# Causal cover of the third and fourth query tile: from PE's cover products to one VectorE call with the row maximum

## The chip, the cores and the metric

The kernel runs on one core of one Trainium2 chip. The metric is the device time of one execution in microseconds (us). Before the change the three timed runs gave 1072.38, 1071.35 and 1063.21 us, median 1071.35 us.

## The reference, cut to what matters

The program computes one layer over 8 batches of 512 tokens with 128 features: a Mamba2 block with a residual and a layer norm, then causal attention with 16 heads of width 8, then a mixture of eight experts with two chosen per token, and layer norms. The change touches the scores of the attention alone:

```
scores = jnp.einsum('bhqd,bhkd->bhqk', q, k) / jnp.sqrt(jnp.float32(hd))
causal = jnp.tril(jnp.ones((s, s), bool))
scores = jnp.where(causal, scores, jnp.finfo(scores.dtype).min)
attn = jax.nn.softmax(scores, axis=-1)
```

A query row may look at itself and at earlier keys. The softmax needs the largest allowed score of each row, and this maximum is what the changed code finds.

## The kernel before, in words

The stages follow one another with barriers between them: the Mamba stage, the projection to queries, keys and values, attention (`attention_layer`, about 326 to 797 us of the profile), the experts and the last norms. `layer` calls them in this order.

In attention a batch has 512 queries, which are 4 query tiles of 128, and 16 heads in 4 groups of four. The scores are computed twice. First the **maximum pass**: PE multiplies 128 queries of one head with the keys up to the end of their tile, into one of four PSUM banks (`S_BANK`), and VectorE takes the maximum along each row into `mx`. `MAX_UNITS` lists the work of a pass, 11 units for each group of heads: tile 0 is one unit of four heads (4 times 128 columns), tile 1 two units of two heads (2 times 256), tiles 2 and 3 four units each with one head (384 and 512 columns). A pass has 44 units (`NMAX`), of which 32 have one head. Then, after all 44, PE transposes the maxima (`max_rows`, line 1619), VectorE splits them into three bf16 parts (lines 1429 to 1436), and SyncE stores these parts by DMA into rows of `qx` (`store_max`, line 1168). Second the **exponential pass** of the same batch: PE multiplies again, transposed and with the maxima as more rows (line 1632), ScalarE takes the exponential (line 1353), GpSimd sets what the causal mask forbids to zero (line 1313), PE multiplies with the values (`pv`, line 1647).

`SCHEDULE` sets the order of all engines around this: 44 slots, one unit of the exponential pass of a batch in each, and between them, up to slot 35, the units of the maximum pass of the *next* batch. Further steps of the batch *before* have slots of their own, among them its layer norm (lines 1453 to 1469) and the choice of its experts (`choose`, lines 1480 to 1528, a chain of 21 small VectorE instructions in slots 21 to 32, each of which waits for the one before; PE's `ranks`, line 1688, waits for one of them). Slot 36 holds the transposition of the maxima. Every engine works through its own queue in order and waits at semaphores.

The maximum pass of batch 0 stands alone in front of the loop and uses six banks instead of four. The seven other passes are woven into the exponential passes of batches 0 to 6. The exponential pass of batch 7 has no maximum pass beside it.

A unit's cover: for each head PE adds a second product to the block on the diagonal (line 1614), the 128 by 128 identity times `hide`, which holds -3e38 above the diagonal and zero elsewhere. So the forbidden scores are hidden before VectorE's `tensor_reduce` (line 1417) sees them. PE waits in front of unit u of a pass until VectorE has done unit u-4 (`mx_ready`), so that the bank is free.

In the loop an instruction that has to wait carries a wait on a register's value. `wait_apart` puts the wait into an instruction of its own, with a semaphore increment behind it.

Of the kernel before, what the change touches and what calls it, by code (L numbers as in the profile page):

```python
# [5 lines left out]
BF16 = mybir.dt.bfloat16  # L6
U32 = mybir.dt.uint32
ALU = mybir.AluOpType
# [3 lines left out]
P = 128  # L12
BATCH, SEQ, D = 8, 512, 128
# [35 lines left out]
def wait_apart(eng, sem, value, passed):  # L49

    eng.wait_ge(sem, value)
    eng.sem_inc(passed, 1)
# [786 lines left out]
QK_ROWS = PARTS * PARTS * DH  # L839
# [157 lines left out]
NMAX, NEXP, STEPS = len(MAX_UNITS), len(EXP_UNITS), GROUPS * TILES  # L997
# [46 lines left out]
def attention_layer(nc, x1_dram, q_parts, k_parts, v_dram, w_o, g1, b1, wg, w1, w2, slots, h_all, gates, table, w1s, w2s):  # L1044
# [6 lines left out]
    with ExitStack() as ctx:  # L1051
        def sb(name, shape, dt=F32):
            return ctx.enter_context(nc.sbuf_tensor(name, shape, dt))

        def pair(name, shape, dt=F32):
            return [sb(f"{name}{p}", shape, dt) for p in range(2)]

        def sem(name):
            sems.append(nc.alloc_semaphore(name))
            return sems[-1]  # L1060
# [5 lines left out]
        ident = sb("ident_c", [P, P])  # L1066
        ident16 = sb("ident16", [P, P], BF16)
        hide = sb("hide", [P, P], BF16)
        minus_half = sb("minus_half_c", [P, TILES])
        qx = pair("qx", [96, AH, SEQ], BF16)  # L1070
        kx = pair("kx", [96, AH, SEQ], BF16)
# [3 lines left out]
        mx = sb("mx", [P, AH, TILES])  # L1075
# [37 lines left out]
        ps = ctx.enter_context(nc.psum_tensor("psB", [P, 8, 512], F32))  # L1113
        S_BANK, E_BANK, PV_BANK, MISC = 0, 4, 6, 7

        S_BANKS, E_BANKS, FIRST_BANKS = 4, 2, 6

        w_loaded, consts, vx_made = sem("wo_loaded"), sem("att_constants"), sem("vx_made")
        kones_made, kones_loaded = sem("kones_made"), sem("kones_loaded")
        qk_loaded, v_loaded, vx_ready = [[sem(f"qk_loaded{p}_{g}") for g in range(GROUPS)] for p in range(2)], [sem(f"v_loaded{p}") for p in range(2)], sem("vx_ready")  # L1120
        s_ps, mx_ready = sem("s_ps"), sem("mx_ready")
# [14 lines left out]
        pool_passed, dve_passed, pe_passed = sem("pool_passed_c"), sem("dve_passed_c"), sem("pe_passed_c")  # L1136
# [4 lines left out]
        def times(it, p):  # L1141

            return it + p // 2 + 1
# [87 lines left out]
        def spread_v(pool, it, p):  # L1231
            q = p % 2
            wait_apart(pool, v_loaded[q], times(it, p) * 16, pool_passed)
            nc.gpsimd.tensor_copy(vx[q][:, :, :, 0:DH], vtok[q][:, :, :].rearrange("p t (h d) -> p t h d", d=DH)).then_inc(vx_ready, 1)

        @block.gpsimd
        def _(pool):
# [5 lines left out]
                                    pattern=[[-1, P]], channel_multiplier=1).then_inc(consts, 1)  # L1243
            nc.gpsimd.affine_select(out=ident16[:, :], in_=ones[:, :], compare_op=ALU.is_equal, fill=0.0, base=0,
                                    pattern=[[-1, P]], channel_multiplier=1).then_inc(consts, 1)
            nc.gpsimd.affine_select(out=hide[:, :], in_=hide[:, :], compare_op=ALU.is_gt, fill=0.0, base=0,
                                    pattern=[[1, P]], channel_multiplier=-1).then_inc(consts, 1)
            pool.wait_ge(vx_made, 2)
            spread_v(pool, 0, 0)
            nc.gpsimd.memset(ones16[:, :], 1.0).then_inc(route_consts, 1)  # L1250
# [5 lines left out]
                                    pattern=[[1, P]], channel_multiplier=-1).then_inc(route_consts, 1)  # L1256
# [76 lines left out]
            for e in range(E):  # L1333
                nc.gpsimd.indirect_dma_start(out=slots, out_offset=bass.IndirectOffsetOnAxis(ap=fill_idx[:, e:e + 1], axis=0),
                                             in_=filler[:, :], in_offset=None, bounds_check=SLOTS - 1,
# [69 lines left out]
        def _(dve):  # L1405
# [7 lines left out]
            def max_unit(row, u, banks=S_BANKS):  # L1413
                qt, h0, heads = MAX_UNITS[u]
                width = (qt + 1) * P
                dve.wait_ge(s_ps, row(NMAX, u + 1))
                nc.vector.tensor_reduce(mx[:, h0:h0 + heads, qt],  # L1417
                                        ps[:, S_BANK + u % banks, 0:heads * width].rearrange("p (h n) -> p h n", n=width),
                                        AX.X, ALU.max).then_inc(mx_ready, 1)
# [53 lines left out]
            def choose(it, p, i):  # L1473
# [53 lines left out]
                    ins = v.tensor_tensor(gates[:, 1, row_tiles(it, p)], gates[:, 0, row_tiles(it, p)], ex[:, :], ALU.mult)  # L1527
                ins.then_inc(chosen, 1)

            for u in range(NMAX):  # L1530
                max_unit(Row(0, 0), u, FIRST_BANKS)
            max_rows(Row(0, 0), 0, 0)
# [42 lines left out]
            for e in range(E):  # L1575
# [14 lines left out]
                                        op0=ALU.mult, op1=ALU.add))  # L1590
# [7 lines left out]
        def _(pe):  # L1598
            pe.wait_ge(consts, 6)

            def max_unit(row, it, p, u, banks=S_BANKS):

                qt, h0, heads = MAX_UNITS[u]
                q, width = p % 2, (qt + 1) * P
                if u % (NMAX // GROUPS) == 0:
                    pe.wait_ge(qk_loaded[q][h0 // 4], times(it, p) * QK_LOADS)
                n = row(NMAX, u + 1 - banks)
                if not isinstance(n, int) or n > 0:
                    pe.wait_ge(mx_ready, n)
                for j in range(heads):  # L1610
                    out = ps[:, S_BANK + u % banks, j * width:(j + 1) * width]
                    nc.tensor.matmul(out, qx[q][0:QK_ROWS, h0 + j, qt * P:(qt + 1) * P],  # L1612
                                     kx[q][0:QK_ROWS, h0 + j, 0:width], start=True, stop=False)
                    ins = nc.tensor.matmul(out[:, qt * P:width], ident16[:, :], hide[:, :], start=False, stop=True)  # L1614
                ins.then_inc(s_ps, 1)
# [608 lines left out]
def layer(nc, X, W_in, conv_w, conv_b, dt_bias, A_log, Dskip, norm_w, W_out,  # L2224
          w_qkv, w_o, g1, b1, wg, w1, bb1, w2, bb2, g2, b2, out):

    def dram(name, shape, dt=F32):
        return nc.dram_tensor(name, shape, dt, kind="Internal").ap()

    x1 = dram("x1_rows", (BATCH, SEQ, D))  # L2230
    q_parts = dram("q_parts", (BATCH, PARTS, D, SEQ), BF16)
    k_parts = dram("k_parts", (BATCH, PARTS, D, SEQ), BF16)
    v = dram("v_rows", (BATCH, SEQ, D))
    slots = dram("slots", (SLOTS, PAY))
    results = dram("results", (RESULTS, D))

    mamba_layer(nc, X, W_in, conv_w, conv_b, dt_bias, A_log, Dskip, norm_w, W_out, x1)
    qkv_projection(nc, x1, w_qkv, q_parts, k_parts, v)
    with ExitStack() as kept:
        gates = kept.enter_context(nc.sbuf_tensor("gates", [P, TOPK, ALL_TILES], F32))  # L2240
        table = kept.enter_context(nc.sbuf_tensor("table", [1, 3, SLOT_TILES], U32))
        h_all = kept.enter_context(nc.sbuf_tensor("h_all", [P, ALL_TILES, D], F32))
        w1s = kept.enter_context(nc.sbuf_tensor("w1s", [P, E * F], F32))
        w2s = kept.enter_context(nc.sbuf_tensor("w2s", [P, E * F], F32))
        attention_layer(nc, x1, q_parts, k_parts, v, w_o, g1, b1, wg, w1, w2, slots, h_all, gates, table, w1s, w2s)
        x1s = kept.enter_context(nc.sbuf_tensor("x1s", [P, ALL_TILES, D], F32))
        experts(nc, slots, w1s, bb1, w2s, bb2, table, results, x1, b2, x1s)
        last_norms(nc, x1s, h_all, results, gates, g2, out)
# [22 lines left out]
```

## Time and profile before

| what | us |
|---|---|
| median of three runs | 1071.35 |
| the profiled execution | 1066.94 |
| its span, first to last instruction | 1065.3 |
| PE busy over the span | 759.3 |
| VectorE busy over the span | 652.5 |
| ScalarE busy over the span | 505.2 |
| GpSimd busy over the span | 394.0 |
| all cover products on PE (512) | 113.1 |
| all row maxima of 512 columns with one head (128) | 82.5 |
| all row maxima of 384 columns (128) | 65.6 |

Matmuls overlap in PE's pipeline, so the busy time of a group is not what it takes from the queue: the distance from one start to the next is. The same holds for VectorE, in a smaller measure. "Idle before" is charged to the instruction that had to wait, with the engine and line that released it.

### The profile page before, as it was taken

What the parts mean: (1) busy time and instruction counts of PE and PEld (TensorE: products, weight loads), DVE (VectorE), ACT (ScalarE), POOL (GpSimd) and SP (SyncE); (2) the same over time, 40 slices, a digit from 0 to 9 for tenths busy, and PEclk for the clock granted to TensorE, in tenths of its full rate; (3) what the DMA queues carried; (4) which work ended last, traced back from release to release, by engine and by line L of the source; (5) the groups of instructions that cost most, each with busy time, mean ns of one, the idle gap of its engine ahead of it and who ended that gap; (6) DMA issues with size and microseconds to landing.
All of it is one profiled execution on the core that took longest, in us unless ns stands there. A gap on an engine that the chain in (4) does not pass through costs nothing. (4 is left out here: it accounts for less than half of the span.)

```text
span 1065.3 us, 21410 instructions
## 1 busy us (share of the span) xinstructions
PE 759.3 (71%) x5297; PEld 506.3 (48%) x5298; DVE 652.5 (61%) x1639; ACT 505.2 (47%) x987; POOL 394.0 (37%) x500
## 2 busy tenths in 40 slices
PE   5788887777564589989788979898820799998000
PEld 3565666555342334535354434443320699998000
DVE  3888887885355546768486938692231355554485
ACT  3556555552260035556455635555500566765134
POOL 1223332233200012353435343545535355555254
PEclk9989988987695558999899969997855799999555
DMA  1000000000284311344424232301201332221231
GB/s 43 16 21 26 25 15 14 25 15 11 89 264 150 120 33 47 86 104 98 119 65 111 74 100 66 96 24 50 65 30 38 88 85 72 82 83 32 82 114 43
DMA packets 87086, 72.38 MB, mean 68 GB/s; under 512 B 10932, under 2 KB 78139, under 8 KB 87007
## 3 DMA queue, kind: packets, MB, share of 16 engines
q1 hardware_dynamic: 81726, 60.29, 20.4%
q0 software_dynamic: 5280, 11.13, 3.3%
q8 instruction: 39, 0.64, 0.3%
q14 instruction: 41, 0.33, 0.1%
HBM read 44.05 MB, written 22.12 MB: 62 GB/s over the span
## 5 line engine op out<-in xcount | busy, mean ns | idle before, releaser
L1353 ACT ACTIVATE pb<-psB 128x512 f32<-128x512 f32 (+1 forms) x352 | 187.2, 558 | 205.9 <-PE psB L1632 175.5
L1417 DVE TENSOR_REDUCE mx<-psB 128x1 f32<-128x384 f32 (+3 forms) x352 | 209.4, 635 | 108.8 <-PE psB L1614 105.8
L1612 PE MATMUL psB<-kx,qx 72*128 72x384 bf16 (+3 forms) x512 | 150.3, 344 | 21.7 <-DMA kx<-k_parts 21.7
L1632 PE MATMUL psB<-qx,kx 75*128 75x256 bf16 (+3 forms) x512 | 136.0, 326 | 37.4 <-DMA qx<-mparts 18.4
L1313 POOL TENSOR_SCALAR_AFFINE_SELECT pb<-pb 128x512 f32<-128x512 f32 x128 | 81.3, 641 | 185.8 <-ACT pb L1353 184.5
L1647 PE MATMUL psB<-pb,vx 128*32 128x512 f32 (+3 forms) x1024 | 107.2, 494 | 14.1 <-POOL pb L1313 14.1
L1614 PE MATMUL psB<-hide,ident 128*128 128x128 bf16 x512 | 113.1, 244 | 0.0
L1632 PEld LDWEIGHTS psB<-qx,kx 75*128 75x128 bf16 x512 | 45.5, 103 | 123.3 <-issue 62.6
L1883 POOL DMA_INDIRECT results<-y_e,dest x72 | 70.1, 974 | 77.7 <-DVE y_e L1950 39.1
L1943 DVE TENSOR_TENSOR pre<-psE,biases 128x512 f32<-128x512 f32 x72 | 49.8, 692 | 55.8 <-PE psE L1981 42.6
L1989 PE MATMUL psE<-w2s,gT 128*128 x576 | 80.0, 282 | 2.9 <-ACT gT L1912 1.4
L1300 POOL DMA_INDIRECT slots<-pay,idx x64 | 64.3, 1005 | 45.3 <-DVE den_r L1523 14.9
L1981 PE MATMUL psE<-hT_e,w1t 128*128 128x128 f32 x576 | 77.6, 279 | 0.3 <-ACT hT_e L1907 0.3
L1612 PEld LDWEIGHTS psB<-kx,qx 72*128 72x128 bf16 x512 | 56.7, 111 | 41.2 <-issue 25.2
L1989 PEld LDWEIGHTS psE<-w2s,gT 128*128 128x128 f32 x576 | 69.7, 191 | 7.4 <-issue 6.2
L277 POOL TENSOR_TENSOR ra<-upto,a 128x512 f32<-128x512 f32 x32 | 34.5, 1090 | 104.2 <-DVE a L515 104.2
L1981 PEld LDWEIGHTS psE<-hT_e,w1t 128*128 128x128 f32 x576 | 71.1, 195 | 0.9 <-ACT hT_e L1907 0.7
L1614 PEld LDWEIGHTS psB<-hide,ident 128*128 128x128 bf16 x512 | 57.6, 112 | 21.0 <-issue 7.4
L1902 ACT ACTIVATE w1t<-w1s 128x512 f32 x72 | 45.4, 630 | 44.3 <-DMA biases<-in_L_ffn_bb 38.9
L1912 ACT ACTIVATE gT<-pre 128x512 f32<-128x512 f32 x72 | 45.4, 630 | 37.8 <-DVE pre L1943 22.3
L481 DVE SCALAR_TENSOR_TENSOR acc<-psA,cw,acc 128x509 f32<-128x509 f32 (+2 forms) x72 | 53.7, 746 | 5.1 <-ACT acc L348 3.4
L201 PE MATMUL psA<-xdt,mm 128*128 128x64 f32 x256 | 36.8, 291 | 20.7 <-DVE mm L549 20.7
(246 smaller groups left out, 1328.6 us busy)
## 6 DMA issues: line engine op xcount, KB each, us to landing
qx<-q_parts SPq DMA_DIRECT2D x96, 96.0 KB
kx<-k_parts SPq DMA_DIRECT2D x96, 96.0 KB
hin<-slots SPq DMA_DIRECT2D x72, 64.5 KB
ys<-results SPq DMA_DIRECT2D x16, 256.0 KB, 3.0
q_parts<-qpart SPq DMA_DIRECT2D x8, 384.0 KB
k_parts<-kpart SPq DMA_DIRECT2D x8, 384.0 KB
xin<-in_L_attn_X SPq DMA_DIRECT2D x8, 256.0 KB
x_rows<-x1o SPq DMA_DIRECT2D x8, 256.0 KB
```

Of the source, the lines that this page charges most:

```text
L481: ins = nc.vector.scalar_tensor_tensor(out=acc[:, c, s:SEQ], in0=bank(6 + c % 2)[:, 0:SEQ - s], scalar=cw[:, c, k:k + 1], in1=acc[:, c, s: ...
L1300: nc.gpsimd.indirect_dma_start(out=slots, out_offset=bass.IndirectOffsetOnAxis(ap=idx[q][:, k, t:t + 1], axis=0), in_=pay[k][q][:, t, :], ...
L1313: nc.gpsimd.affine_select(out=pb[step % PBUF][:, :, 0:P], in_=pb[step % PBUF][:, :, 0:P], compare_op=ALU.is_ge, fill=0.0, base=0, pattern= ...
L1353: nc.scalar.activation(pb[step % PBUF][:, h0:h0 + heads, 0:width], src, ACT.Exp).then_inc(exp_ready, 2 if u == NEXP - 1 else 1)
L1417: nc.vector.tensor_reduce(mx[:, h0:h0 + heads, qt], ps[:, S_BANK + u % banks, 0:heads * width].rearrange("p (h n) -> p h n", n=width), AX. ...
L1612: nc.tensor.matmul(out, qx[q][0:QK_ROWS, h0 + j, qt * P:(qt + 1) * P], kx[q][0:QK_ROWS, h0 + j, 0:width], start=True, stop=False)
L1614: ins = nc.tensor.matmul(out[:, qt * P:width], ident16[:, :], hide[:, :], start=False, stop=True)
L1632: ins = nc.tensor.matmul(ps[:, E_BANK + u % E_BANKS, j * width:(j + 1) * width], kx[q][0:MAX_ROWS, 4 * g + h0 + j, kt * P:(kt + 1) * P], q ...
L1647: ins = nc.tensor.matmul(ps[32 * j:32 * (j + 1), PV_BANK, kt * P:SEQ], vx[q][:, kt, 4 * g + j, :], pb[step % PBUF][:, j, 0:width], start=( ...
L1883: nc.gpsimd.indirect_dma_start(out=results, out_offset=bass.IndirectOffsetOnAxis(ap=dest[tile.ring][:, 0:1], axis=0), in_=y[tile.ring][:, ...
L1981: ins = nc.tensor.matmul(ps[:, UP_BANK + tile.pair, c * P:(c + 1) * P], w1t[tile.pair][:, c * P:(c + 1) * P], hT[tile.pair][:, :], start=T ...
L1989: ins = nc.tensor.matmul(ps[:, Y_BANK + tile.pair, 0:D], gT[tile.pair][:, c, :], w2s[:, bass.ds(at + c * D, D)], start=(c == 0), stop=(c = ...
```

## The change

For the units with one head (query tiles 2 and 3) PE no longer adds the cover product: there is one matmul per unit, which ends the accumulation. VectorE's `tensor_reduce` is replaced by `tensor_tensor_reduce`, which adds `cover` to the scores, writes the sums as bf16 to a scratch tile `covered`, and gives the maximum of the sums in `mx`. `cover` is a new fp32 tile of 128 by 512 in SBUF, zero where a key is allowed and -3e38 elsewhere, of which the last 384 or all 512 columns are read. GpSimd makes it at the stage's start. Its wait on PE becomes a `wait_apart`. Units with four or two heads are unchanged, so `hide` stays.

```diff
+        cover = sb("cover", [P, SEQ])
...
+        covered = [sb(f"covered{k}", [P, SEQ], BF16) for k in range(FIRST_BANKS)]
...
+            nc.gpsimd.memset(cover[:, :], 0.0).then_inc(cover_made, 1)
+            pool.wait_ge(cover_made, 1)
+            nc.gpsimd.affine_select(out=cover[:, :], in_=cover[:, :], compare_op=ALU.is_ge, fill=-3e38, base=SEQ - P,
+                                    pattern=[[-1, SEQ]], channel_multiplier=1).then_inc(cover_made, 1)
             pool.wait_ge(vx_made, 2)
...
             def max_unit(row, u, banks=S_BANKS):
                 qt, h0, heads = MAX_UNITS[u]
                 width = (qt + 1) * P
+                if heads == 1:
+                    wait_apart(dve, s_ps, row(NMAX, u + 1), dve_passed)
+                    nc.vector.tensor_tensor_reduce(out=covered[u % banks][:, 0:width], in0=ps[:, S_BANK + u % banks, 0:width],
+                                                   in1=cover[:, SEQ - width:SEQ], scale=1.0, scalar=-3e38, op0=ALU.add, op1=ALU.max,
+                                                   accum_out=mx[:, h0, qt:qt + 1]).then_inc(mx_ready, 1)
+                    return
...
+            dve.wait_ge(cover_made, 2)
             for u in range(NMAX):
                 max_unit(Row(0, 0), u, FIRST_BANKS)
...
                     pe.wait_ge(mx_ready, n)
+                if heads == 1:
+                    nc.tensor.matmul(ps[:, S_BANK + u % banks, 0:width], qx[q][0:QK_ROWS, h0, qt * P:(qt + 1) * P],
+                                     kx[q][0:QK_ROWS, h0, 0:width], start=True, stop=True).then_inc(s_ps, 1)
+                    return
```

On VectorE, in the loop, among the steps that choose the experts of the batch before (`lg`, `m`, `key` and `kmax` belong to that choice; REGISTER_ALU computes the value that a wait compares with), there stood before:

```order
L1416 REGISTER_ALU
L1417 TENSOR_REDUCE mx<-psB 128x1
L1480 REGISTER_ALU
L1495 SCALAR_TENSOR_TENSOR lg<-sel,lg 128x32
L1480 REGISTER_ALU
L1498 TENSOR_REDUCE m<-lg 128x4
L1416 REGISTER_ALU
L1417 TENSOR_REDUCE mx<-psB 128x1
```

The same place with the change (line 1425 is the new call, 1508 and 1511 are the two steps of the choice):

```order
L51 REGISTER_ALU
L1425 ISA covered,mx<-psB,cover 128x512
L1425 ISA mx 128x1
L1493 REGISTER_ALU
L1508 SCALAR_TENSOR_TENSOR lg<-sel,lg 128x32
L1493 REGISTER_ALU
L1511 TENSOR_REDUCE m<-lg 128x4
L51 REGISTER_ALU
L1425 ISA covered,mx<-psB,cover 128x512
L1425 ISA mx 128x1
```

The order of the steps is the same. One call stands as two instructions on VectorE: one that reads the scores and `cover`, and one that has no input and writes `mx`.

On PE at the same slots (line 1632 is a product of the exponential pass) there stood before:

```order
L1609 REGISTER_ALU
L1612 MATMUL psB<-kx,qx 128x512
L1614 MATMUL psB<-hide,ident 128x128
L1630 REGISTER_ALU
L1632 MATMUL psB<-qx,kx 128x384
L1609 REGISTER_ALU
L1612 MATMUL psB<-kx,qx 128x128
L1614 MATMUL psB<-hide,ident 128x128
```

and with the change:

```order
L1623 REGISTER_ALU
L1625 MATMUL psB<-kx,qx 128x512
L1648 REGISTER_ALU
L1650 MATMUL psB<-qx,kx 128x384
L1623 REGISTER_ALU
L1630 MATMUL psB<-kx,qx 128x128
L1632 MATMUL psB<-hide,ident 128x128
```

The product with `hide` is gone behind the 512-column unit and stays behind the 128-column ones; nothing else moved.

## Rows read from the trace of the kernel before

**Rows 1.** The page: busy time over the span, and PE's granted clock by slices.

```profile
PE 759.3 (71%) x5297; PEld 506.3 (48%) x5298; DVE 652.5 (61%) x1639; ACT 505.2 (47%) x987; POOL 394.0 (37%) x500
PEclk9989988987695558999899969997855799999555
```

**Rows 2.** Busy time in stretches: start:end, length, then each engine, clock, DMA.

```profile
core 0: us, PE busy (x) PEld busy (x) DVE busy (x) ACT busy (x) POOL busy (x), PEclk, DMA share, GB/s
573.00:614.60 41.60, 37.94 (x342) 20.49 (x342) 33.78 (x84) 23.35 (x46) 17.89 (x24) 0.96 0.38 98
626.00:672.60 46.60, 43.45 (x341) 22.46 (x341) 34.07 (x84) 22.96 (x46) 14.11 (x20) 0.83 0.30 80
377.00:421.20 44.20, 43.96 (x284) 21.62 (x285) 27.56 (x48) 21.05 (x39) 8.16 (x13) 0.67 0.12 35
```

**Rows 3.** Timeline of VectorE, 573 to 615 us: start, length, instruction, [idle before].

```profile
584.23 1.29 DVE L1417 TENSOR_REDUCE mx<-psB 128x1 f32<-128x512 f32 x2 [0.91 <-PE psB L1614]
596.76 1.29 DVE L1417 TENSOR_REDUCE mx<-psB 128x2 f32<-128x512 f32 x2 [0.39 <-PE psB L1614]
598.63 0.56 DVE L1417 TENSOR_REDUCE mx<-psB 128x1 f32<-128x384 f32 x1 [0.58 <-PE psB L1614]
603.48 0.19 DVE L1489 TENSOR_TENSOR key<-key,rank 128x32 f32<-128x32 f32 x1
603.59 1.28 DVE L1417 TENSOR_REDUCE mx<-psB 128x1 f32<-128x512 f32 x2
608.33 0.56 DVE L1417 TENSOR_REDUCE mx<-psB 128x1 f32<-128x384 f32 x1 [0.55 <-PE psB L1614]
611.98 2.47 DVE L1417 TENSOR_REDUCE mx<-psB 128x1 f32<-128x512 f32 x4
```

**Rows 4.** Timeline of PE at the end of the same pass.

```profile
612.28 0.22 PE L1614 MATMUL psB<-hide,ident 128*128 128x128 bf16 x1
614.60 0.27 PE L1619 MATMUL psB<-ident_c,mx 128*64 128x128 f32 x1 [0.38 <-issue]
```

**Rows 5.** Timeline of PE from the maxima of the pass before to the next exponentials.

```profile
567.42 0.27 PE L1619 MATMUL psB<-ident_c,mx 128*64 128x128 f32 x1 [0.38 <-DVE mx L1417]
573.06 0.39 PE L1632 MATMUL psB<-qx,kx 75*128 75x512 bf16 x1 [0.75 <-DMA qx<-mparts]
```

**Rows 6.** Timeline of PE: a cover product at the full clock, then at half of it.

```profile
603.20 0.22 PE L1614 MATMUL psB<-hide,ident 128*128 128x128 bf16 x1
603.26 0.33 PE L1632 MATMUL psB<-qx,kx 75*128 75x384 bf16 x1
...
382.09 0.31 PE L1614 MATMUL psB<-hide,ident 128*128 128x128 bf16 x1
382.20 0.53 PE L1612 MATMUL psB<-kx,qx 72*128 72x384 bf16 x1
```

**Rows 7.** Timeline, first pass: VectorE's last step, SyncE's stores, PE's first exponential.

```profile
362.12 0.28 DVE L1436 TENSOR_TENSOR mparts<-mrest,mparts 64x128 bf16<-64x128 f32 x1
364.62 0.43 SPq L1162 DMA_DIRECT2D vtok<-v_rows  x1
365.09 4.41 SPq L1168 DMA_DIRECT2D qx<-mparts  x3
377.24 0.59 PE L1632 MATMUL psB<-qx,kx 75*128 75x512 bf16 x1 [16.05 <-DMA qx<-mparts]
```

**Rows 8.** Timeline of VectorE: two-source instructions of 512 columns, PSUM with SBUF.

```profile
317.48 0.68 DVE L952 SCALAR_TENSOR_TENSOR qrest<-psB,qpart 128x512 f32<-128x512 f32 x1
318.08 0.68 DVE L952 SCALAR_TENSOR_TENSOR krest<-psB,kpart 128x512 f32<-128x512 f32 x1
```

**Rows 9.** Timeline of ScalarE in the Mamba stage: sums read out of its accumulator.

```profile
54.97 0.19 ACT L408 ACTIVATION_READ_ACCUMULATOR sq<-y 128x1 f32 x1
55.19 0.42 ACT L408 ACTIVATE sq<-y 128x256 f32<-128x256 f32 x1
55.52 0.19 ACT L408 ACTIVATION_READ_ACCUMULATOR sq<-y 128x1 f32 x1
55.61 1.00 ACT L413 ACTIVATE yT<-psA 128x1024 f32<-128x1024 f32 x1
```

**Rows 10.** Timeline at the stage's start: GpSimd's last constant, and VectorE's first maxima.

```profile
326.94 0.29 POOL L1246 TENSOR_SCALAR_AFFINE_SELECT hide<-hide 128x128 bf16<-128x128 bf16 x1
336.20 24.45 DVE L1417 TENSOR_REDUCE mx<-psB 128x4 f32<-128x512 f32 x44 [4.93 <-PE psB L1614]
```

**Rows 11.** Timeline of VectorE: an instruction behind a wait that stands apart (line 1460).

```profile
586.27 0.87 DVE L1457 BATCH_NORM_STATS2 bst_c<-r_c 128x6 f32<-128x128 f32 x4
587.28 0.38 DVE L1462 BATCH_NORM_AGGREGATE mv_c<-bst_c 128x2 f32<-128x6 f32 x4
```

More of the change, by code:

```diff
@@ L1116, in attention_layer @@
         S_BANKS, E_BANKS, FIRST_BANKS = 4, 2, 6
+        covered = [sb(f"covered{k}", [P, SEQ], BF16) for k in range(FIRST_BANKS)]
         w_loaded, consts, vx_made = sem("wo_loaded"), sem("att_constants"), sem("vx_made")
+        cover_made = sem("cover_made")
         kones_made, kones_loaded = sem("kones_made"), sem("kones_loaded")
```

## The prediction

> **What bounds the kernel now.** I read the page first. Over the span no engine is full [rows 1], so the change has to be judged stage by stage. It lies in attention, and there I asked for busy time by stretches, one for each maximum pass in the loop. A typical pass runs from a first exponential at 573.06 to the transposition of the maxima at 614.60 [rows 4, 5]. In these 41.6 us PE is busy 37.94 and VectorE 33.78 [rows 2]: near each other, with ScalarE and GpSimd far behind. A PE busy 91% looks like the bound, but a matmul's record is longer than its place in the queue, so I went on to VectorE's timeline. Up to 584.23 it waits for PE again and again, the last time for 0.91 us. In the 30 us from there to the end it waits three times, 0.39, 0.58 and 0.55 us, 1.52 together [rows 3]. At the end PE has finished the last unit's cover by 612.50, while VectorE still has four reduces from 611.98 to 614.45. PE's transposition starts at 614.60, behind VectorE, after only 0.38 us of idleness of its own [rows 3, 4]. The reader is to see that **VectorE sets the end of the pass, with PE close behind**. What follows hangs on that end: from transposition to the next batch's first exponential it is 5.64 us, the last part of it a wait for the stored maxima [rows 5]. A microsecond more on VectorE before the transposition is a microsecond more in the kernel.
>
> **The sum, part by part.** Per pass 32 units change.
>
> *PE's cover products go.* Start to start one takes 0.06 us at the full clock and 0.11 at half [rows 6]. In the typical pass they are 32 x 0.06 = 1.9 us, but not of the path: PE's work already ends before VectorE's. There I count nothing for them beyond fewer waits of VectorE (below). In the first pass of the loop, 377 to 421 us, PE is busy 43.96 of 44.20 and VectorE only 27.56 [rows 2]. This one is PE's. Half of its changed units run at the low clock, half after the clock has risen: 16 x 0.11 + 16 x 0.06 = **-2.7 us**.
>
> *VectorE's main instruction.* Four reduces of 512 columns last 2.47 us with 0.68 for the last, so 0.60 from start to start [rows 3]. Two-source instructions of the same width, one source in PSUM, one in SBUF, also start 0.60 apart [rows 8]. I take no difference, and 0.02 as its upper end.
>
> *VectorE's second instruction*, the reading of the accumulator into `mx`, is new: the call is not one instruction but two. VectorE does no such reading in this trace. The nearest rows: a small VectorE instruction of 32 columns delays the reduce behind it by 0.11 [rows 3]. The 128 columns between 384 and 512 make some 0.12 (records of 0.56 and 0.68), so 32 columns are 0.03 of it and one column leaves **0.08**. ScalarE does read an accumulator. There 0.22 passes from the reading's start to the next instruction where that waits for it, 0.09 where it does not [rows 9]. So 0.22 is my upper end. The lower is zero, since records of 0.68 already overlap by 0.08. I take 0.08, because the next unit's main instruction waits for nothing of the reading.
>
> The Trainium skill ("Vector Engine (DVE) Microarchitecture Reference", Measured stream behaviour on trn2) gives about 75 ns per instruction beside the columns. By that the sum below would be about 0.6 us smaller, so it would not change sign.
>
> *The wait that stands apart.* Behind the one VectorE has before (line 1460), 0.14 us lie between the end of the statistics and the next start [rows 11], where reduces whose scores are there follow without a gap. In the dense part the wait is met before its turn comes and runs beside the streaming instruction, so nothing. Where VectorE waits for PE it may add 0.1, and there it has slack. If it were paid in the dense part it would act like a larger second instruction.
>
> *A typical pass.* Six of the 32 changed units lie before 584.23 and vanish in waits for PE. The 26 behind it lengthen VectorE by 26 x 0.08 = 2.1 us. Against this stand the 1.52 us of waits. Part of them stays, since PE comes late there for steps that themselves wait for VectorE (norm and choice of the batch before), so I let half, 0.8, absorb. That is **+1.3 us**. Five passes are of this kind (2, 3, 4, 5 and 7): **+6.5 us**. Pass 6 (626 to 672.6) ran in part at a low clock and has VectorE idle for 46.60 - 34.07 = 12.5 us [rows 2]. Its second half is as dense as the others, so I take **+0.5**.
>
> *The first pass, alone, is covered.* VectorE runs 44 reduces without a break [rows 10] and would take 32 x 0.08 = 2.6 us longer. But its last step ends at 362.40, and SyncE stores the maxima only at 365.09, after the loads of batch 1 queued ahead. That is 2.7 us of cover. Then the stores land at 377, behind those loads' traffic [rows 7]. **0**. GpSimd's two instructions for `cover` start at 327.2, nine microseconds before the first reduce [rows 10]. A quarter of that work took 0.29, so it is free. The added wait passes at once.
>
> Sum: -2.7 + 6.5 + 0.5 = **+4.3 us**. Against the profiled execution (1066.9) that is 1071. That execution lies 4.4 us under the median and about 1.6 under the mean of all four times shown (1068.5), and I put the kernel on that mean: **1073 us**.
>
> **The rivals.**
>
> *The reading waits for its predecessor to drain (slower).* Then each unit costs 0.22, and 0.02 for the main one: 26 x 0.24 - 0.8 = 5.4 us per pass, 27 for five, about 3 for pass 6, -2.7 for the PE pass, and 32 x 0.24 - 2.7 = 5.0 in the first pass, most of it still behind the loads: +27 to +32, or 1096 to 1101. The place is the dense half of each pass. For it: ScalarE's rows with the wait. Against: those without. With a cost c per unit the change reaches +1% (10.7 us, about what a measurement of this kernel can tell from no change) at c near 0.13. The Trainium skill ("VectorE: DVE Perf Modes", The DRAIN you can't avoid) says the next instruction does not start until the pipe is empty, and its rules advise few instructions. That speaks against this change. Records of 0.68 that start 0.60 apart disagree in part, and no row here shows it for a reading. Chance that the cost is large enough, between 0.13 and 0.24: **0.36**.
>
> *PE sets the passes (faster).* Then every product counts: 32 x 0.06 = 1.9 in five passes, 2.4 in pass 6, 2.7 in the PE pass, 14.7 us in all: 1054. For it: 91% busy. Against: VectorE's dense half and the last reduce. The skill ("Trainium Kernel Development and Optimization", Performance Expectations) calls PE's matmul time a bad measure and its weight loads a good one; these are 20.49 of 41.60 [rows 2], on the side of the forecast. Chance **0.07**.
>
> *The clock.* Pass 6 took 46.6 us at a granted 0.83 where typical ones take 41.6 at 0.96 [rows 2]. One such pass more or less moves the total by 5 us, either way. With a small second cost this alone could reach -1%. Chance of being decided by it **0.07**, half to each side.
>
> **How the numbers follow.** The forecast with costs up to 0.13 keeps 0.50, all within 1%. Faster: 0.07 from PE and 0.03 from the clock, **0.10**. Slower: 0.36 and 0.04, **0.40**. Same **0.50**. The range leaves out the PE case and the top of the draining case: with no cost of the second instruction, passes shorten by some 0.5 us each and the sum is about -6, so **1062**. Above, a cost of 0.19 gives 5 x 4.1 + 2 - 2.7 = +20, and with a little of the clock **1093**.
>
> **What would show it.** In the changed profile the new instruction's rows give the second instruction's cost directly: start of the main one, start of the reading, start of the next. Expected: 0.68, then 0.08 to the next. VectorE's busy time in a typical pass should rise by some 2.5 us and its waits for PE shrink. PE should show waits for `mx`, in front of scores or of the transposition. The distance from one transposition to the next should grow from 47.2 to about 48.5 us in passes without a loop's end. The pass at 377 us should be shorter by 2.7, and the first exponential should stay at 377. The forecast is wrong if VectorE shows long waits in the second half, or if a reading holds the next unit by much over 0.1 us.

## The result, and the profile after

The changed kernel takes 1082.07 us (median of 16 executions, 1075.02 to 1098.78), the kernel before 1066.90 us beside it (16 executions). The ratio is **1.0164, 95% interval 1.0127 to 1.0201**: slower by more than the 1% that can be told from no change. The profiled execution took 1075.43 us. (Medians are taken over all executions, ratios leave out those far above the fastest of their kernel, so a ratio need not be the quotient of two medians.)

The page of the changed kernel, the two lines that answer to [rows 1]:

```profile
PE 773.9 (72%) x5041; PEld 492.2 (46%) x5042; DVE 657.3 (61%) x1895; ACT 504.7 (47%) x987; POOL 394.5 (37%) x502
PEclk8899898897785589989587959796765799999555
```

PE has 256 instructions fewer and is busy 15 us *longer*: its clock is lower in more of the slices. The stretches that answer to [rows 2], in the same columns (from a pass's first exponential to its transposition):

```profile
572.70:618.50 45.80, 39.30 (x314) 19.02 (x313) 35.00 (x116) 24.67 (x49) 17.71 (x24) 0.91 0.33 90
624.40:676.20 51.80, 47.79 (x314) 22.26 (x313) 34.91 (x116) 24.33 (x48) 18.15 (x24) 0.73 0.31 82
373.80:407.10 33.30, 33.00 (x252) 15.45 (x252) 27.13 (x80) 20.93 (x40) 8.11 (x13) 0.87 0.17 47
```

The typical pass takes 45.8 us where it took 41.6. VectorE's busy time grew by 1.2 us only (33.78 to 35.00). The next pass stands at a clock of 0.73. The pass at 374 is far shorter than before, but its clock is also higher in this execution (0.87 against 0.67), so how much of that the change did cannot be told.

VectorE among the steps of the choice, the place that answers to [rows 3] (start, length, instruction):

```profile
600.13 0.19 DVE L1498 TENSOR_REDUCE m<-lg 128x4 f32<-128x32 f32 x1
600.38 0.56 DVE L1425 CUSTOM_DVE_ANT_0 covered<-psB,cover 128x384 bf16<-128x384 f32 x1
600.87 0.08 DVE L1425 DVE_READ_ACCUMULATOR2_ANT mx<- 128x1 f32 x1
600.87 0.56 DVE L1425 CUSTOM_DVE_ANT_0 covered<-psB,cover 128x384 bf16<-128x384 f32 x1
601.34 0.09 DVE L1425 DVE_READ_ACCUMULATOR2_ANT mx<- 128x1 f32 x1
601.34 0.19 DVE L1500 TENSOR_TENSOR key<-lg,m 128x32 f32<-128x32 f32 x1
601.56 0.19 DVE L1502 TENSOR_TENSOR key<-key,rank 128x32 f32<-128x32 f32 x1
601.81 0.56 DVE L1425 CUSTOM_DVE_ANT_0 covered<-psB,cover 128x384 bf16<-128x384 f32 x1
...
616.50 0.68 DVE L1425 CUSTOM_DVE_ANT_0 covered<-psB,cover 128x512 bf16<-128x512 f32 x1
617.11 0.08 DVE L1425 DVE_READ_ACCUMULATOR2_ANT mx<- 128x1 f32 x1
617.11 0.68 DVE L1425 CUSTOM_DVE_ANT_0 covered<-psB,cover 128x512 bf16<-128x512 f32 x1
```

Two things are to be seen. First, the reading of the accumulator lasts 0.08, but the next main instruction starts *with* it: calls of 512 columns start 0.61 apart, reduces did so at 0.60. **The second instruction costs 0.01 us, not 0.08.** Second, a changed unit behind a small instruction starts 0.25 after that one (600.13 to 600.38, 601.56 to 601.81), where it was 0.11 in [rows 3] (603.48 to 603.59).

The Trainium skill ("VectorE: DVE Perf Modes", The DRAIN you can't avoid) says that the next operation does not start until the pipe is empty, and adds that one that is not held starts earlier. The prediction named only the first half. The trace agrees with the second: records of 0.68 start 0.61 apart, and the next call starts together with the reading of 0.08.

PE waits longer for the choice of the experts. First the kernel before, then the changed one: the product with the counts, and a group of eight products with the values behind it; in the changed kernel also the transposition that answers to [rows 4].

```profile
605.95 0.19 PE L1688 MATMUL psB<-cnt,before 128*128 128x40 bf16 x1 [1.39 <-DVE cnt L1502]
606.68 1.07 PE L1647 MATMUL psB<-pb,vx 128*32 128x512 f32 x8
```

```profile
607.62 0.19 PE L1706 MATMUL psB<-cnt,before 128*128 128x40 bf16 x1 [2.21 <-DVE cnt L1515]
608.58 1.93 PE L1665 MATMUL psB<-pb,vx 128*32 128x512 f32 x8
618.55 0.39 PE L1637 MATMUL psB<-ident_c,mx 128*64 128x128 f32 x1 [1.24 <-DVE mx L1425]
```

The pause in front of the count product is 1.39 us before and 2.21 after, in each of the six passes at full work. It grew by 0.82. On the way to the counts five changed units of 384 or 512 columns stand behind a small step of the choice (600.38 is the first): 5 x 0.14 = 0.7 of it. The same eight products then take 1.93 in place of 1.07. The clock shows it, in the columns of [rows 2]: the pause, the 4 us behind it, two stretches of 24 us behind a transposition, and all passes of the loop. First the kernel before, with the 4 us behind the pause of one more pass (662.30), then the changed one:

```profile
604.60:606.00 1.40, 0.05 (x2) 0.06 (x3) 1.33 (x6) 0.15 (x1) 0.00 (x0) 1.00 1.16 221
606.00:610.00 4.00, 4.00 (x40) 2.55 (x41) 3.27 (x11) 2.22 (x5) 0.64 (x1) 1.00 0.15 39
662.30:666.30 4.00, 4.00 (x25) 1.67 (x26) 1.78 (x6) 0.93 (x3) 0.64 (x1) 0.57 0.11 32
615.00:639.00 24.00, 16.76 (x96) 7.86 (x98) 7.45 (x17) 9.12 (x18) 9.05 (x11) 0.64 0.38 100
515.50:539.50 24.00, 16.93 (x136) 9.12 (x134) 10.27 (x23) 11.02 (x22) 10.51 (x14) 0.86 0.40 103
370.00:745.00 375.00, 319.24 (x2600) 163.60 (x2601) 248.16 (x609) 195.89 (x385) 150.55 (x198) 0.88 0.29 77
```

```profile
605.40:607.60 2.20, 0.00 (x1) 0.00 (x0) 2.13 (x9) 0.00 (x0) 0.00 (x0) 1.00 0.72 159
607.60:611.60 4.00, 3.98 (x24) 1.78 (x25) 1.77 (x6) 1.13 (x3) 0.64 (x1) 0.57 0.09 25
619.00:643.00 24.00, 23.27 (x112) 10.33 (x111) 9.15 (x28) 9.36 (x18) 9.33 (x12) 0.52 0.37 92
509.50:533.50 24.00, 23.28 (x109) 10.23 (x107) 9.04 (x27) 9.35 (x18) 9.42 (x13) 0.51 0.37 94
370.00:745.00 375.00, 331.99 (x2329) 152.63 (x2329) 249.00 (x820) 190.30 (x375) 146.03 (x193) 0.80 0.28 75
```

Behind the first pause of 1.39 us PE is granted the full 2.4 GHz, behind the one of 2.21 mostly 1.2 GHz. The kernel before has the full clock in five of its six such passes; in the sixth, at 662 us, the same pause is followed by 0.57. The changed kernel has 0.57 to 0.73 in all six.

Two stretches of 24 us in the changed kernel stand at 1.2 GHz nearly throughout (0.51, 0.52). They lie behind two of the seven transpositions in the loop; behind the other five it has 0.57 to 0.93. The kernel before has 0.64 to 0.93 in the seven. The mean of the seven is 0.70, where it was 0.86. Over the seven passes the granted clock is 0.80 against 0.88. The kernel before was profiled once; the two other profiles of the changed one (e4 and f9 below) have 0.51 and 0.52 behind the same two transpositions.

The first pass of the stage, alone, in the changed kernel, answers to [rows 7] and [rows 10]:

```profile
324.60 0.61 POOL L1253 TENSOR_SCALAR_AFFINE_SELECT cover<-cover 128x512 f32<-128x512 f32 x1
332.67 1.90 DVE L1430 TENSOR_REDUCE mx<-psB 128x4 f32<-128x512 f32 x3 [4.65 <-PE psB L1632]
357.51 0.39 PE L1637 MATMUL psB<-ident_c,mx 128*64 128x128 f32 x1 [2.88 <-DVE mx L1425]
361.88 3.99 SPq L1171 DMA_DIRECT2D qx<-mparts  x3
373.72 0.59 PE L1650 MATMUL psB<-qx,kx 75*128 75x512 bf16 x1 [15.82 <-DMA qx<-mparts]
```

GpSimd has `cover` ready 7.5 us before the first maximum. From the first maximum to the transposition it is 24.84 us, before 24.59 (336.20 to 360.79). The stage began 3.5 us earlier in this execution, and the stores and the first exponential moved with it.

### The profile page after: what moved, and what is told of

Same layout as the page of the kernel before. It is cut to its first block and busy times, and to the rows that moved or that the text cites. A ratio compares the mean times of both kernels' runs of the same rounds, so it can differ in the third digit from the quotient of the medians.

```text
span 1073.8 us, 21414 instructions
## 1 busy us (share of the span) xinstructions
PE 773.9 (72%) x5041; PEld 492.2 (46%) x5042; DVE 657.3 (61%) x1895; ACT 504.7 (47%) x987; POOL 394.5 (37%) x502
## 5 line engine op out<-in xcount | busy, mean ns | idle before, releaser
L1425 DVE CUSTOM_DVE_ANT_0 covered<-psB,cover 128x384 bf16<-128x384 f32 (+1 forms) x256 | 149.3, 620 | 42.8 <-PE psB L1625 39.9
L1650 PE MATMUL psB<-qx,kx 75*128 75x256 bf16 (+3 forms) x512 | 145.9, 354 | 21.7 <-DMA qx<-mparts 17.5
L1665 PE MATMUL psB<-pb,vx 128*32 128x512 f32 (+3 forms) x1024 | 119.4, 545 | 11.9 <-POOL pb L1320 11.8
L1430 DVE TENSOR_REDUCE mx<-psB 128x2 f32<-128x512 f32 (+1 forms) x96 | 62.9, 686 | 66.7 <-PE psB L1632 66.4
L1650 PEld LDWEIGHTS psB<-qx,kx 75*128 75x128 bf16 x512 | 48.6, 108 | 119.0 <-issue 66.4
L1625 PE MATMUL psB<-kx,qx 72*128 72x384 bf16 (+1 forms) x256 | 94.7, 418 | 1.1 <-DVE mx L1430 0.7
L1630 PE MATMUL psB<-kx,qx 72*128 72x128 bf16 (+1 forms) x256 | 55.4, 283 | 24.5 <-DMA kx<-k_parts 21.9
L1632 PE MATMUL psB<-hide,ident 128*128 128x128 bf16 x256 | 51.8, 249 | 0.0
```

What stands on the lines that cost most here:

```text
L1425: nc.vector.tensor_tensor_reduce(out=covered[u % banks][:, 0:width], in0=ps[:, S_BANK + u % banks, 0:width], in1=cover[:, SEQ - width:SEQ] ...
L1430: nc.vector.tensor_reduce(mx[:, h0:h0 + heads, qt], ps[:, S_BANK + u % banks, 0:heads * width].rearrange("p (h n) -> p h n", n=width), AX. ...
L1625: nc.tensor.matmul(ps[:, S_BANK + u % banks, 0:width], qx[q][0:QK_ROWS, h0, qt * P:(qt + 1) * P], kx[q][0:QK_ROWS, h0, 0:width], start=Tru ...
L1650: ins = nc.tensor.matmul(ps[:, E_BANK + u % E_BANKS, j * width:(j + 1) * width], kx[q][0:MAX_ROWS, 4 * g + h0 + j, kt * P:(kt + 1) * P], q ...
L1665: ins = nc.tensor.matmul(ps[32 * j:32 * (j + 1), PV_BANK, kt * P:SEQ], vx[q][:, kt, 4 * g + j, :], pb[step % PBUF][:, j, 0:width], start=( ...
```

## The experiments

Two theories at first. **A**: less work on PE keeps its clock low, wherever the pauses are. **B**: VectorE's calls delay the choice of the experts, PE pauses there, and that costs. The table has all runs. The pause is PE's wait at the count product in the profiled execution; "clock" is the mean granted clock of all executions of the run, that of the kernel before, run beside it, in brackets.

| run | median us (before) | ratio, interval | pause | clock (before) |
|---|---|---|---|---|
| e1, products off | 1058.64 (1070.22) | 0.985, 0.980 to 0.990 | 1.55 | 0.813 (0.821) |
| e2, call on | 1085.23 (1070.22) | 1.012, 1.007 to 1.017 | 2.12 | 0.807 (0.821) |
| e3, wait apart only | 1075.14 (1070.22) | 1.004, 0.999 to 1.009 | 1.77 | 0.815 (0.821) |
| e4, the change | 1086.18 (1070.22) | 1.012, 1.007 to 1.017 | 2.21 | 0.791 (0.821) |
| e5, change, choice earlier | 1065.36 (1074.72) | 0.987, 0.980 to 0.994 | none | 0.817 (0.818) |
| e6, before, choice earlier | 1070.24 (1074.72) | 1.001, 0.996 to 1.006 | none | 0.820 (0.818) |
| e7, change, pause filled | 1068.63 (1074.72) | 0.993, 0.989 to 0.998 | 0.48 | 0.822 (0.818) |
| e8, change but for one group | 1066.43 (1074.72) | 0.992, 0.988 to 0.997 | 1.39 | 0.814 (0.818) |
| f9, the change | 1082.16 (1071.12) | 1.010, 1.005 to 1.015 | 2.21 | 0.789 (0.820) |
| f10, before, pause longer | 1092.46 (1071.12) | 1.019, 1.013 to 1.025 | 2.20 | 0.807 (0.820) |
| f11, before, pause filled | 1067.98 (1071.12) | 0.993, 0.988 to 0.998 | none | 0.824 (0.820) |
| f12, e8 with pause filled | 1063.80 (1071.12) | 0.994, 0.990 to 0.999 | none | 0.817 (0.820) |

**e1, the removal alone.** PE's cover products of the one-head units go, VectorE keeps its reduces. So the maxima of tiles 3 and 4 are taken without the mask.

```diff
+                if heads == 1:
+                    nc.tensor.matmul(ps[:, S_BANK + u % banks, 0:width], ..., start=True, stop=True).then_inc(s_ps, 1)
+                    return
                 for j in range(heads):
```

> The kernel before with only PE's half of the change: no cover products for the one-head units, VectorE's reduce as it was. It leaves the causal mask out of the maxima of the third and fourth query tile. Theory A (less work on PE keeps its clock low): the mean granted clock falls from about 0.83 to about 0.80 as in the changed kernel, with stretches of 10 to 24 us at the low clock behind each pass's start, and the time rises by 0.5 to 1.5%. Theory B (VectorE's new call makes the steps behind it late, PE pauses, and only that costs): PE's wait for the choice of the experts stays at 1.4 us, the clock stays at 0.83 and the time falls, by between 0 and 1.3% (14 us if PE sets the passes).

Measured: 1.5% faster. That is against A, and a little more than B allowed. The products did cost something, though VectorE sets the end of the pass. The clock did fall somewhat (0.813 against 0.821).

**e2, the call alone.** The changed kernel without that block: VectorE makes the new call, PE still adds its products.

> The kernel before with only VectorE's half of the change: the new call with the wait apart, and PE's cover products still there (their sums are covered twice). Theory A: the clock stays at about 0.83, and the time rises by no more than what VectorE's delays cost directly, 0.8 us in each of six passes, so 0.2 to 0.6%. Theory B: everything that the changed kernel lost is here: PE waits 2.2 us for the choice in place of 1.4, the clock falls to 0.80, the time rises by 1.5% or more, since the products come on top.

Measured: 1.2% slower, with a pause of 2.12 us: between what A and B allowed. Nearly the whole loss comes with VectorE's side, and PE's missing products are not needed for it.

**e3, only the wait apart.** Reduces and products as before, the wait of a one-head unit in an instruction of its own.

```diff
-                dve.wait_ge(s_ps, row(NMAX, u + 1))
+                if heads == 1:
+                    wait_apart(dve, s_ps, row(NMAX, u + 1), dve_passed)
+                else:
+                    dve.wait_ge(s_ps, row(NMAX, u + 1))
```

> The kernel before, where only the wait of the one-head reduces stands apart with its increment; same reduce, same products. If the 0.14 us that a unit behind a small VectorE instruction now starts later comes from the wait apart, it shows here too: 0.25 us from a small step's start to the reduce behind it, where the kernel before has 0.11, PE waits some 2.2 us for the choice, time up by 0.3 to 0.8%. If it comes from the call being two instructions, the distances stay at 0.11 and the time is that of the kernel before within 0.3%.

The time cannot be told from no change. Its VectorE gives the price of the wait alone, though, as start, length, instruction:

```profile
550.89 0.19 DVE L1488 TENSOR_REDUCE m<-lg 128x4 f32<-128x32 f32 x1
551.10 1.02 DVE L1420 TENSOR_REDUCE mx<-psB 128x1 f32<-128x384 f32 x2
```

0.21 behind a small instruction, where 0.11 stood before and 0.25 with the whole change: neither of the two distances that were expected. So of the 0.14 per such unit 0.10 is the wait apart and 0.04 the call. The pause follows: 1.39, 1.77, 2.21. A version with the wait inside the call was not tried.

**e4**, the changed kernel again beside these three:

> The changed kernel once more, on the same chip and against the same runs of the kernel before. Both theories expect its ratio again, 1.013 to 1.020, with a granted clock of 0.78 to 0.80.

The loss stands, at the lower end of what was expected. The removal gains 12 us alone, the call costs 15 alone, and together they cost 16 here, not 3. That sum does not close by work alone.

**e5, the choice earlier in the changed kernel**, so that the counts are there when PE asks.

```diff
-CHAIN_AT = [21 + i // 2 for i in range(14)] + [29, 29, 30, 30, 31, 31, 32]
+CHAIN_AT = [21 + i // 3 for i in range(14)] + [29, 29, 30, 30, 31, 31, 32]
```

> The changed kernel with one size altered: the first 14 steps of the choice of experts stand three to a slot (slots 21 to 25) in place of two (21 to 27). PE meets its step of the choice at the same slot as before, so the counts it waits for should be there in time. Theory B (VectorE's slower choice steps hold PE at that step, 2.2 us per pass against 1.4, and that pause costs time and clock): PE's wait in front of the count product falls under 0.5 us, the passes shorten by 1 to 2 us each, seven passes, and the time is 7 to 14 us less than the changed kernel's, 1.000 to 1.005 of the kernel before. Theory A (less work on PE keeps its clock low, wherever the pause stands): the wait goes, another comes, and the ratio stays at 1.010 to 1.016.

The pause is gone and the loss with it, against A; the gain is larger than B expected (1.000 to 1.005). The profiled execution was granted 0.799, less than the mean of its run (0.817), so its passes are not typical.

**e6**, the same edit in the kernel before:

> The control: the kernel before, with the same earlier choice steps and nothing else. Theory B: its own wait of 1.39 us at the count product goes as well, worth up to 7 us: ratio 0.993 to 1.0. Theory A says nothing for it: 1.0. If the earlier steps only push row maxima back and PE then waits for banks, 1.0 to 1.005.

No difference that can be told. So the edit is not a gain of its own: it helps where the pause is 2.2 us, not where it is 1.4.

**e7, the pause filled in the changed kernel.** The counts come no earlier, PE only has work meanwhile.

```diff
+                pe.wait_ge(chosen, row(CHAIN, 1))
+                for _ in range(8):
+                    nc.tensor.matmul(ps[:, MISC, :].rearrange("p (t n) -> p t n", n=P), ident16[:, :],
+                                     ones16[:, :].unsqueeze(1).broadcast_to([P, TILES, P]), start=True, stop=True)
                 pe.wait_ge(chosen, row(CHAIN, COUNTED))
```

> The changed kernel with work for PE in the pause at the count product: it waits for the first counts of the choice and then multiplies eight times 512 columns (identity by ones) into a bank whose result is overwritten, about 1.8 us at the full clock, 3.5 at half. The results are not used. Theory A (the clock falls because PE does too little): the dip behind the pause goes, the mean granted clock rises from 0.79 toward 0.82, and the time stays the same or falls by up to 10 us, ratio 1.003 to 1.012. Theory B: the pause is filled but not shorter, so nothing is gained, and the filler may run past the pause: 1.012 to 1.02.

Its PE in the pause, and two of its stretches in the columns of [rows 2], the first behind a transposition at 604.50:

```profile
592.66 1.89 PE L1707 MATMUL psB<-ones,ident 128*128 128x512 bf16 x8
595.03 0.19 PE L1710 MATMUL psB<-cnt,before 128*128 128x40 bf16 x1 [0.48 <-DVE cnt L1515]
```

```profile
605.00:629.00 24.00, 20.48 (x162) 9.47 (x161) 14.96 (x48) 13.10 (x25) 12.48 (x17) 0.93 0.43 115
370.00:745.00 375.00, 328.15 (x2551) 154.00 (x2551) 257.17 (x858) 206.46 (x411) 157.94 (x209) 0.92 0.29 79
```

This is the run that decides. PE does work that nobody uses, in the same wait for the same counts, and against the kernel before the ratio is 0.993 where the changed kernel has 1.010 to 1.016: some 2% better. Both theories missed it. B expected no gain at all, and A, which had the clock right, expected at most a return to 1.003. So an idle PE costs there by what follows for the clock, and not only because the counts come late.

The stretches show it larger than it is on average, since this execution was granted 0.836 and the mean of its run is 0.822 (0.790 in the changed kernel). Over the passes it has 0.92 where the changed kernel has 0.80, and 0.93 behind the two transpositions where that one has 0.51 and 0.52; behind the other five it has 0.79 to 1.00.

**e8, one part undone.** The units of the third group of heads, which stand among the steps of the choice, keep reduce and cover product.

```diff
-                if heads == 1:
+                if heads == 1 and h0 // 4 != 2:
```

(on VectorE and on PE)

> One part of the change undone: the units of the third group of heads (8 of the 32 changed ones per pass), which stand in the slots of the choice of experts, go back to reduce and cover product. Theory B (the delay of the choice steps is what costs): VectorE's choice steps no longer meet a changed unit, PE's wait at the count product returns to about 1.4 us, and most of the loss goes: ratio 1.000 to 1.005. Theory A (products missing from PE everywhere): three quarters of the loss stay, 1.008 to 1.012.

The pause is back at 1.39 with three quarters of the change in place, and all of the loss is gone; the result is 0.8% faster than the kernel before, better than B expected too.

**f9**, the changed kernel a third time:

> The changed kernel as it is, beside the other runs of this call: 1.012 to 1.018 of the kernel before, with a granted clock near 0.79, by every theory.

Slower by 1.0%, a little under what was expected.

**f10, the pause alone**, in the kernel before, nothing of the change:

```diff
                 elif i == 12:
+                    for k in range(8):
+                        v.tensor_tensor(spare[:, k, :, :], sel[:, 0, :, :], sel[:, 1, :, :], ALU.add)
```

> The kernel before with a longer pause and nothing of the change: in front of the choice step that makes the counts VectorE does eight more additions of 32 columns (into a spare tile, not used), some 0.11 us each, 0.9 us per pass. PE's wait at the count product grows from 1.39 to about 2.2 us, the changed kernel's. Theory of the pause (a longer idleness of PE there costs granted clock behind it and at the next pass's start): mean clock falls from 0.82 to 0.80 or below, time 1.010 to 1.016. Rival (only VectorE's added time counts, and the change's loss is its slower calls): 7 passes by at most 0.9 us = 6.3 us, 1.003 to 1.006, and the clock stays.

The eight additions go into a spare tile. VectorE and PE at that place, then the stretch behind the pause in the first pass and in this one, and that over the passes:

```profile
604.82 0.89 DVE L1504 TENSOR_TENSOR spare<-sel 128x32 f32<-128x32 f32 x8
605.88 0.22 PE L1691 MATMUL psB<-cnt,before 128*128 128x40 bf16 x1 [2.20 <-DVE cnt L1505]
```

```profile
446.00:450.00 4.00, 4.00 (x40) 2.55 (x41) 3.18 (x11) 2.18 (x5) 0.63 (x1) 1.00 0.11 29
605.90:609.90 4.00, 4.00 (x23) 1.55 (x24) 1.70 (x5) 0.92 (x3) 0.64 (x1) 0.50 0.09 24
370.00:745.00 375.00, 329.93 (x2524) 166.42 (x2524) 248.15 (x642) 187.16 (x368) 143.72 (x190) 0.83 0.28 76
```

0.8 us more of VectorE per pass, 6 us in all, made the kernel 21 us slower by the medians, over three times as much. The 4 us behind the pause are at 1.2 GHz (0.50) in five of the six passes; in the first the clock stays full. The rival that counts only VectorE's time is out: it allowed 1.006. But with the same pause the clock is 0.807, as in e2, and the changed kernel's 0.789 to 0.791: the pause is not all of it.

**f11, the pause filled in the kernel before** (six products in place of eight), the control of e7:

> The control of the filled pause, on the kernel before: PE multiplies six times 512 columns (not used) while it waits for the counts, 1.3 us at the full clock in a wait of 1.39. Theory of the pause: the pause of 1.39 us already costs little clock in this kernel, so a gain of at most 1%: 0.990 to 1.000. Rival (more work on PE in any place raises the clock, and the filled changed kernel gained by that): as large a gain as there, about 2%, 0.98.

A gain of 0.7%. Filler raises the clock here as well, 0.824 against 0.820, but it does not give the 2% that it gives the changed kernel.

**f12**, e8 and this filler together:

> The best version the runs point to: the change for three of the four groups of heads, reduce and cover product kept for the third group, which meets the choice of experts, and the pause of 1.39 us that is left filled with six products of 512 columns. If both effects are of one cause (the pause and the clock behind it) they do not add much: 0.985 to 0.993. If PE's missing products are a loss of their own (clock lower wherever PE has less to do), no better than the two apart, 0.992 to 1.0.

No better than either (e8 0.992, f11 0.993). This result was assigned beforehand to PE's missing products being a loss of their own. The interval, 0.990 to 0.999, reaches the other range as well, so the run does not decide between the two.

**The clock behind the count product, in all traces.** Each has six passes at full work. With a pause of 1.39 to 1.55 us (the kernel before, e1, e8) the 4 us behind it are below the full clock in 2 of 18 passes. With 1.77 to 2.21 us (e2, e3, f10, and the changed kernel three times) they are in 33 of 36, at 0.50 to 0.73. With 0.48 us or none (e6, e7, f11, f12) they are in none of 24. One trace does not fit: e5 has no pause there and still 0.50 to 0.65 in four of six passes. In each of its passes PE waits some 0.70 and 0.50 us for maxima just in front. So the pause at the product lowers the clock, and is not the only thing that does. Nor does each such dip show in the time: e3 has five of them, and its time cannot be told from the kernel before.

**An account with the clock.** The executions of one kernel differ mainly by the granted clock: the kernel before took 1057.99 us at a mean of 0.833 and 1091.25 at 0.795, and over the 29 executions beside f9 the slope is 8.1 us per 0.01 (7.9 beside e1 to e4, 8.0 beside e5 to e8). By that slope, as an estimate: in f9 the clock is lower by 0.031, worth +25 us; measured are +11 (medians), so the rest of the change is worth -14. For e4 the same gives +24 and +16, a rest of -8. For e1 it is +6 and -12, a rest of -18; for e8 +3 and -8, a rest of -12; for e5 +1 and -9, a rest of -10. For f12 it is +3 and -7, a rest of -10. In these six runs, which all leave products out, the rest is 8 to 18 us *less*. With the call and all products (e2) it is +12 and +15, a rest of +3. The clock would so take most of the surplus out of the sum that e4 left open: -18 and +3 make -15, where the whole change has -14 and -8. The other five fit less well or say nothing: e7, the whole change, is -3 and -6, a rest of only -3, with its filler in it; f10 is +11 and +21, a rest of +10 where VectorE's added work is 6; e3, e6 and f11 have rests of 0, -3 and 0. All this rests on a correlation within kernels and is argued, not shown.

## Why the prediction came out as it did

The range 1062 to 1093 held 1082.07. The likeliest case, no change by 1%, did not come: it is slower by 1.6%. Slower had 0.40, but nearly all of it (0.36) for a mechanism that was not at work. That the time fell inside the range is luck: the sum gave +4.3 us, and the change cost 11 to 16 us by the medians, through a wait and a clock that are not in the sum. By its steps:

- **What bounds a pass.** That VectorE sets the end was right: PE waits 1.24 us for the last maxima where it stood idle for 0.38. That PE's products therefore count for nothing in a typical pass was wrong. e1 gained 12 us, close to the 14.7 of the rival "PE sets the passes", which had 0.07. VectorE waits for PE up to 584.23 in the prediction's own reading of the pass, so a gain on PE can pass through that part. That this is the way is argued; no run separates the parts of a pass.
- **The second instruction** at 0.08 us, 26 per pass: measured 0.01 (mains 0.61 apart). The bounds 0 to 0.22 held it, the choice of the nearest row did not. The draining rival (0.22, chance 0.36) is refuted by the same rows. The bound of 0.02 on the main instruction held.
- **The wait apart "in the dense part ... nothing": the step that failed.** Behind a small instruction it costs 0.10, and the call 0.04 more, which makes five units x 0.14 = 0.7 us in front of the counts, of the 0.82 by which the pause grew. The text had the row for it (0.14 behind the statistics) and looked for who waits only at the end of the pass. The one who waits is PE, at the count product, in the middle.
- **A typical pass +1.3**, transposition to transposition 47.2 to 48.5: measured 51.7 (566.87 to 618.55). What is missing from the sum is the clock.
- **The clock** as a rival with 0.07 and 5 us either way, by chance. It decides, and not by chance: f10 lengthens the pause alone and the clock falls from 0.820 to 0.807; e7 fills it and the clock rises from the changed kernel's 0.790 to 0.822. f11, the same filler where the pause is 1.39, gives 0.004.
- **The pass at 377, -2.7**, cannot be judged: this pass went from 44.2 to 33.3 us, with its clock at 0.67 and then at 0.87. **The first pass, alone, at nothing**: right, but without need of its cover, as it grew by 0.25 us only. **`cover` on GpSimd, free**: right.

The Trainium skill ("TensorE: Matmul & The Clock Gate", A second HAM failure mode: psum-queue depth-cycling) tells of a kernel in which PE idles a little, again and again, between groups of matmuls, so that its clock goes down and up and the throughput suffers. The trace agrees in kind, with one pause per pass in place of many: 2.2 us, then mostly 1.2 GHz (0.57 and 0.50). The section gives no size for it. It would have given the prediction a rival with the right sign.

**What stays open.** Why the changed kernel's clock (0.79) is lower than f10's (0.807) at the same pause: its PE has fewer products, but e1, with as few and a pause of 1.55, has 0.813. Against the kernel before e1 loses 0.008 and e2, with the long pause and all products, 0.014; the change loses 0.030. The two together seem to do more than the sum, and no run separates how. Nor is it shown why the low clock lasts 24 us at the starts of some passes, and why filling a pause ten microseconds earlier shortens it. Such a start is not found in the changed kernel alone: e8 has one at 0.57 and is faster than the kernel before.

## What to carry to other kernels

When an edit slows small steps on one engine, look for every engine that waits for their chain, in the middle of a stage too, and not only at its end. Price a longer pause of PE by the clock that is granted behind it, not by its length alone: here 0.8 us more per pause cost some 3 us per pass. And a partial change can beat the whole one: with the cover moved to VectorE except where VectorE already carries a chain that PE waits for, the kernel is 0.8% (0.3 to 1.2) faster than before, where the whole change is 1.0 to 1.6% slower.

## What the hardware showed that was not expected

- VectorE's reading of its accumulator lasts 0.08 us but delays the next instruction by 0.01: calls of 512 columns start 0.61 apart, of 384 columns 0.47 (600.87 to 601.34).
- A wait in an instruction of its own costs 0.10 us behind an instruction of 32 columns (0.21 against 0.11), and nothing between two reduces (two of 384 columns in 1.02 us, 0.56 for one, with the wait apart in e3 as without it in the kernel before).
- Behind a pause of PE of 1.77 to 2.21 us the next 4 us stood at a granted clock of 0.50 to 0.73 in 33 of 36 passes, behind one of 1.39 to 1.55 us below the full clock in 2 of 18.
- Useless matmuls in a pause made a kernel faster: 0.993 of the kernel before (e7), where the same kernel without them is 1.010 to 1.016.
